# Flamingo block on one core: half of the probabilities of tiles 6 to 30 transposed by DMA

## The reference

```python
def xattn(x, context):                       # x: (2, 2048, 512), context: (2, 77, 384)
    q = (layernorm(x) @ Wq), k = context @ Wk, v = context @ Wv      # 16 heads of 32
    scores = einsum('bhid,bhjd->bhij', q, k) * 32 ** -0.5            # masked by context_mask
    return (softmax(scores) @ v).reshape(B, N, 512) @ Wo
def ffn(x):
    xq = fake_quant(layernorm(x))            # int8 steps, one scale from max |x| of the tensor
    h = fake_quant(silu(xq @ wq(w_gate).T) * (xq @ wq(w_up).T))      # wq: int8 per row
    return h @ wq(w_down).T
x = x + tanh(g_xattn) * xattn(x, ctx)
x = x + tanh(g_ffn) * ffn(x)
```

## Time and profile before

| | |
|---|---|
| median of 3 runs | 635.77 us |
| profiled execution / its span | 635.47 / 633.7 us |
| TensorE, VectorE, ScalarE, GpSimd busy | 612.7, 509.5, 352.0, 193.2 us |
| stretch 190 to 240 us: TensorE, VectorE, ScalarE, GpSimd busy | 50.00, 43.91, 31.83, 17.80 of 50 us |
| granted clock of TensorE, 35 to 375 us | 1.00 |
| TensorE idle from the end of attention to its next weight load at 390.53 us | 4.25 us |

### The profile page before, as it was taken

How to read it: one execution, slowest core, us unless ns; L and a number is a source line. 1 busy time by engine, 2 the same in 40 slices (tenths; PEclk the granted TensorE clock), 3 DMA queues, 4 the chain that set the end, 5 groups by cost and what they waited for, 6 DMA issues and landing times. The chain is left out here.

```text
span 633.7 us, 12623 instructions
## 1 busy us (share of the span) xinstructions
PE 612.7 (97%) x3862; PEld 460.0 (73%) x3862; DVE 509.5 (80%) x954; ACT 352.0 (56%) x512; POOL 193.2 (30%) x416
## 2 busy tenths in 40 slices
PE   8899999999999999999999976999999999899997
PEld 6689999999999999999999864444444444444544
DVE  6588788888988888899888658788888888866764
ACT  5264566667566666756664343555555554365553
POOL 7121233333323333323321202111111110057775
PEclk9999999999999999999999998999999999999999
DMA  8839433222222223222411000276446110099623
GB/s 312 201 94 260 134 59 68 54 62 50 58 67 58 66 58 65 75 43 78 97 49 44 25 0 1 50 242 223 132 136 207 28 29 11 0 345 416 267 110 122
DMA packets 85206, 69.61 MB, mean 110 GB/s; under 512 B 64915, under 2 KB 67373, under 8 KB 85165
## 3 DMA queue, kind: packets, MB, share of 16 engines
q1 hardware_dynamic: 79377, 52.13, 29.8%
q10 hardware_dynamic: 5788, 16.98, 7.6%
HBM read 32.48 MB, written 21.36 MB: 85 GB/s over the span
## 5 line engine op out<-in xcount | busy, mean ns | idle before, releaser
L1342 ACT ACTIVATE sb_silu<-ps_g,sb_sgu 128x512 f32<-128x512 f32 x88 | 60.5, 687 | 72.1 <-PE ps_g L1429 42.7
L1429 PE MATMUL ps_g<-sb_xqT,sb_wgu 128*128 128x512 bf16 x352 | 90.3, 379 | 0.6 <-DVE sb_xqT L1385 0.6
L1429 PE MATMUL ps_u<-sb_xqT,sb_wgu 128*128 128x512 bf16 x352 | 90.3, 379 | 0.0
L1400 DVE SCALAR_TENSOR_TENSOR sb_h<-ps_u,sb_sgu,sb_silu 128x512 f32<-128x512 f32 (+1 forms) x88 | 66.0, 751 | 19.8 <-PE ps_u L1429 19.3
L1053 PE MATMUL ps_o<-sb_vblk,sb_pT 128*128 (+4 forms) x640 | 78.8, 270 | 2.4 <-ACT sb_pT L603 1.6
L1053 PEld LDWEIGHTS ps_o<-sb_vblk,sb_pT 128*128 128x128 f32 (+1 forms) x640 | 76.9, 191 | 3.3 <-ACT sb_pT L603 2.0
L986 PE MATMUL ps_q<-sb_xT_hi,sb_wq_hi 128*128 128x256 f32 x256 | 75.5, 295 | 0.0
L988 PE MATMUL ps_q<-sb_xT_hi,sb_wq_lo 128*128 128x256 f32 x256 | 72.3, 282 | 0.0
L987 PE MATMUL ps_q<-sb_xT_lo,sb_wq_hi 128*128 128x256 f32 x256 | 72.2, 282 | 0.0
L1635 PE MATMUL ps_z<-sb_wdT,sb_hq 128*128 128x512 bf16 x330 | 71.6, 379 | 0.0
L716 DVE TENSOR_REDUCE sb_smax<-ps_s 128x8 f32<-128x616 f32 x64 | 51.1, 798 | 23.6 <-PE ps_s L1031 21.4
(11 more groups left out here) (227 smaller groups left out, 1325.7 us busy)
## 6 DMA issues: line engine op xcount, KB each, us to landing
h_spill<-sb_h SPq DMA_DIRECT2D x4, 2816.0 KB, 8.8
sb_h<-h_spill ACTq DMA_DIRECT2D x16, 704.0 KB, 7.1
out_dram<-sb_wgu SPq DMA_DIRECT2D x31, 256.0 KB, 2.0
sb_x<-in_x_dram ACTq DMA_DIRECT2D x1, 4096.0 KB, 19.4
sb_w_in<-in_L_ffn_w_gate_dram SPq DMA_DIRECT2D x11, 256.0 KB, 2.6
sb_w_in<-in_L_ffn_w_up_dram SPq DMA_DIRECT2D x11, 256.0 KB, 2.6
sb_x<-in_x_dram SPq DMA_DIRECT2D x2, 1024.0 KB, 14.7
sb_x<-in_x_dram SPq DMA_DIRECT2D x2, 512.0 KB, 4.9
```

What stands on the lines that cost most here:

```text
L1342: act.activation(silu[(j * KI + i) % 2][:, :, :].rearrange("p t n -> p (t n)"), p_g[(j * KI + i) % 2][:, :], ACT.Silu, scale=sgu[:, i:i + ...
L1400: dve.scalar_tensor_tensor(steps_h, p_u[(j * KI + i) % 2][:, :, :], sgu[:, KI + i:KI + i + 1], silu[(j * KI + i) % 2][:, :, :], ALU.mult, ...
L1429: last = pe.matmul(banks[(j * KI + i) % 2][:, :], wgu[:, what, k, i * P:(i + 1) * P], xqT[j][:, k, :], start=(k == 0), stop=(k == KD - 1))
```

## The change

For tiles 6 to 30 (`by_dma`) half 0 of the probabilities is not transposed by TensorE. GpSimd splits the 616 words into two planes of 16-bit halves, padded to 640 (`prob_split`, after a small product into `carry`), SyncE transposes the planes with a DMA of 128 x 1280 (`prob_transposed`), and ScalarE joins them into `sb_pT` (`prob_join`). Half 1 stays on TensorE, as do both halves of tiles 0 to 5 and 31, now in two pieces of five transposes instead of three of four, four and two. `sb_prob` has one buffer; the subtraction of half 0 waits for the split of the tile before it. The second half of the outputs goes to a second bank, which it shares with the fifth transpose. On TensorE both halves of the outputs follow both halves of the scores and queries. On VectorE the reduction for the second layer norm moves ahead of the maximum of half 1, and the division of the outputs' first half moves behind the queries' low part. The hardware loop covers slots 8 to 19.

```diff
-CHUNKS = [(0, 4), (4, 8), (8, 2 * KB)]
+PROB0, PROB1 = 6, NT - 1
+PW = KB * P
...
-prob = [sb(f"prob{i}", [P, 2, HW]) for i in range(2)]
-pT = sb("pT", [P, 2 * KB, P])
+prob = sb("prob", [P, 2, HW])
+pT_u = sb("pT", [P, 2 * KB * P * 2], U16)
+pT = pT_u[:, :].bitcast(F32).rearrange("p (k n) -> p k n", n=P)
+ppl_u = sb("ppl", [P, 2, 2 * PW], U16)
...
-p_p = [pb(f"p{i}", [P, 4, P]) for i in range(2)]
+p_pp = pb("p", [P, 8, P])
+p_p = [p_pp[:, 0:4, :], p_pp[:, 4:8, :]]
 p_ob = pb("o", [P, 512])
-p_o = p_ob[:, 0:HH * VW].rearrange("p (h d) -> p h d", h=HH)
+p_o = [a[:, 0:HH * VW].rearrange("p (h d) -> p h d", h=HH)
+       for a in (p_ob, p_pp[:, KB:8, :].rearrange("p k n -> p (k n)"))]
...
+def by_dma(n):
+    return not isinstance(n, int) or PROB0 <= n < PROB1
+def turned(n, half):
+    if by_dma(n):
+        return PROB0 + n + 1
+    return 2 * n + half + 1 - (PROB1 - PROB0 if n >= PROB1 else 0)
...
-        slot(n, n)
-    with eng.Fori(1, 5) as i:
+    for n in range(8):
+        slot(n, n % 4)
+    with eng.Fori(2, 5) as i:
...
+    def prob_transposed(n):
+        if n == PROB0:
+            sp.wait_ge(g_zero, 9)
+        sp.wait_ge(g_ppl, n - PROB0 + 1)
+        sp.wait_ge(a_p, 2 * n)
+        sp.dma_start_transpose(ppl_u[:, 1, :].rearrange("p (c n) -> p c n", n=P),
+                               ppl_u[:, 0, :]).then_inc(d_pT, 16)
...
+    def prob_split(n):
+        wait(pool, a_exp, 2 * n + 1)
+        wait(pool, d_pT, 16 * (n - PROB0))
+        pool.tensor_tensor(carry[:, :], eps[:, :], minus[:, :], ALU.mult)
+        pool.tensor_copy(ppl_planes[:, :, 0:HW], prob_pairs).then_inc(g_ppl, 1)
...
+            pool.wait_ge(t_v, B)
+            pool.memset(ppl_pads, 0.0).then_inc(g_zero, 1)
+        if runs(n, NT) and by_dma(n):
+            prob_split(n)
...
+    def exponential(n, half):
+        wait(act, v_sub, 2 * n + half + 1)
+        act.activation(prob[:, half, :], prob[:, half, :], ACT.Exp, scale=SCALE).then_inc(a_exp, 1)
+    def prob_copy(m, half):
+        wait(act, t_p, turned(m, half))
+        wait(act, t_o, 2 * m - 1 + half)
+        act.copy(pT[:, half * KB:(half + 1) * KB, :], p_pp[:, 0:KB, :]).then_inc(a_p, 1)
+    def prob_join(m):
+        wait(act, d_pT, 16 * (m - PROB0) + 16)
+        wait(act, t_o, 2 * m - 1)
+        act.copy(pT_pairs, ppl_T).then_inc(a_p, 1)
...
-        for c, (k0, k1) in enumerate(CHUNKS):
-            if c == 2 and runs(n - 4, NT - 1):
-                wait(act, g_nb2, n - 3)
-                wait(act, v_xmax, n - 3)
-                if isinstance(n, int) and n >= PLANES_FREE:
-                    act.wait_ge(v_xlo, NT)
-                else:
-                    wait(act, v_x1, n - 2)
-                act.activation(xabs(n - 4), row(n - 4), ACT.Abs, bias=nb2[:, span(n - 4)],
-                               scale=rs2[:, span(n - 4)]).then_inc(a_abs, 1)
-            if runs(n - 1, NT):
-                wait(act, t_p, 3 * (n - 1) + c + 1)
-                wait(act, t_o, 2 * (n - 1) - (c == 0))
-                act.copy(pT[:, k0:k1, :], p_p[c % 2][:, 0:k1 - k0, :]).then_inc(a_p, 1)
-        for half in range(2):
-            if runs(n, NT):
-                wait(act, v_sub, 2 * n + half + 1)
-                act.activation(prob[t % 2][:, half, :], prob[t % 2][:, half, :], ACT.Exp,
-                               scale=SCALE).then_inc(a_exp, 1)
-            if half == 0 and runs(n + 2, NT):
-                q_part(n + 2, (t + 2) % 4)
+        if runs(n - 1, NT):
+            if not by_dma(n - 1):
+                prob_copy(n - 1, 0)
+            prob_copy(n - 1, 1)
+        if runs(n - 4, NT - 1):
+            wait(act, g_nb2, n - 3)
+            wait(act, v_xmax, n - 3)
+            if isinstance(n, int) and n >= PLANES_FREE:
+                act.wait_ge(v_xlo, NT)
+            else:
+                wait(act, v_x1, n - 2)
+            act.activation(xabs(n - 4), row(n - 4), ACT.Abs, bias=nb2[:, span(n - 4)],
+                           scale=rs2[:, span(n - 4)]).then_inc(a_abs, 1)
+        if runs(n, NT):
+            exponential(n, 0)
+        if runs(n - 1, NT) and by_dma(n - 1):
+            prob_join(n - 1)
+        if runs(n + 2, NT):
+            q_part(n + 2, (t + 2) % 4)
+        if runs(n, NT):
+            exponential(n, 1)
...
-        wait(dve, t_p, 3 * (n - 1))
+        if isinstance(n, int) and n == 0:
+            dve.wait_ge(t_ck, 1)
+        elif half == 0 and by_dma(n - 1):
+            wait(dve, g_ppl, n - PROB0)
+        else:
+            wait(dve, t_p, turned(n - 1, half))
         dve.tensor_tensor(
-            prob[t % 2][:, half, :].rearrange("p (g h m) -> p g h m", g=2, h=HG), half_scores(),
+            prob[:, half, :].rearrange("p (g h m) -> p g h m", g=2, h=HG), half_scores(),
...
+        dve.reciprocal(rden[:, half, :], p_o[half][:, :, HD]).then_inc(v_rec, 1)
...
         dve.tensor_tensor(o_sb[:, half * HH * HD:(half + 1) * HH * HD]
-                          .rearrange("p (h d) -> p h d", h=HH), p_o[:, :, 0:HD],
+                          .rearrange("p (h d) -> p h d", h=HH), p_o[half][:, :, 0:HD],
...
             dve.bn_aggr(mvt[:, :], bn2[:, 0, :]).then_inc(v_st2, 1)
-        if runs(n - 1, NT):
-            outputs_rec(n - 1, 0)
+        if runs(n - 4, NT):
+            wait(dve, a_abs, n - 3)
+            dve.tensor_reduce(xmax[:, span(n - 4)], xabs(n - 4), X, ALU.max).then_inc(v_xmax, 1)
+        if runs(n, NT):
+            scores_max(n, 1)
         if runs(n, NW):
...
             dve.reciprocal(w_inv[:, :], w_am[:, :]).then_inc(v_winv, 1)
-        if runs(n - 1, NT):
-            outputs_norm(n - 1, 0)
         if runs(n, NT):
-            scores_max(n, 1)
+            scores_sub(n, t, 1)
         if runs(n, NW):
...
         down_part(n, 1)
-        if runs(n - 4, NT):
-            wait(dve, a_abs, n - 3)
-            dve.tensor_reduce(xmax[:, span(n - 4)], xabs(n - 4), X, ALU.max).then_inc(v_xmax, 1)
-        if runs(n, NT):
-            scores_sub(n, t, 1)
         if isinstance(n, int) and n == 0:
...
             dve.wait_ge(v_v, 2 * B)
-            dve.memset(p_p[1][:, 0, :], 0.0).then_inc(v_zero, 1)
+            dve.memset(p_pp[:, KB - 1, :], 0.0).then_inc(v_zero, 1)
...
         if runs(n - 1, NT):
+            outputs_rec(n - 1, 0)
+            outputs_norm(n - 1, 0)
...
-        wait(pe, a_exp, 2 * n + (1 if c == 0 else 2))
-        wait(pe, a_p, 3 * n + (0, -1, 1)[c])
+    def prob_transpose(n, half):
+        wait(pe, a_exp, 2 * n + half + 1)
+        wait(pe, a_p, 2 * n + (half and not by_dma(n)))
+        wait(pe, v_o, 2 * n)
         if isinstance(n, int) and n == 0:
             pe.wait_ge(v_zero, 1)
-        k0, k1 = CHUNKS[c]
-        for k in range(k0, k1):
-            half, j = divmod(k, KB)
-            last = pe.transpose(p_p[c % 2][0:ROWS[j], k - k0, :],
-                                prob[t % 2][:, half, P * j:P * j + ROWS[j]], identf[:, :])
+        for j in range(KB):
+            last = pe.transpose(p_pp[0:ROWS[j], j, :], prob[:, half, P * j:P * j + ROWS[j]],
+                                identf[:, :])
         last.then_inc(t_p, 1)
...
     def outputs(n, half):
-        wait(pe, a_p, 3 * n + 2 + half)
-        wait(pe, v_o, 2 * n + half)
+        wait(pe, a_p, 2 * n + (2 if by_dma(n) else 1 + half))
+        wait(pe, v_o, 2 * n - 1 + half)
         b = n // (S // P)
...
             last = pe.matmul(
-                p_o[:, first:end + 1, :].rearrange("p h d -> p (h d)"),
+                p_o[half][:, first:end + 1, :].rearrange("p h d -> p (h d)"),
...
-        prob_transpose(n - 1, (t - 1) % 4, 0)
-        prob_transpose(n - 1, (t - 1) % 4, 1)
+        prob_transpose(n - 1, 0)
         out_transpose(n - 2)
         project(n - 3, [0])
-        prob_transpose(n - 1, (t - 1) % 4, 2)
+        prob_transpose(n - 1, 1)
...
         if runs(n - 1, NT):
-            prob_transpose(n - 1, (t - 1) % 4, 0)
-            prob_transpose(n - 1, (t - 1) % 4, 1)
+            prob_transpose(n - 1, 1 if by_dma(n - 1) else 0)
         if runs(n + 2, NT):
             queries(n + 2, (t + 2) % 4, 0)
-        if runs(n - 1, NT):
-            outputs(n - 1, 0)
-            prob_transpose(n - 1, (t - 1) % 4, 2)
-        if runs(n, NT):
+        if runs(n - 1, NT) and not by_dma(n - 1):
+            prob_transpose(n - 1, 1)
+        early = isinstance(n, int) and n < 2
+        if early:
             scores(n, t, 1)
...
             queries(n + 2, (t + 2) % 4, 1)
+        if runs(n, NT) and not early:
+            scores(n, t, 1)
         if runs(n - 1, NT):
+            outputs(n - 1, 0)
```

More of the change, by code:

```diff
@@ L93, in flamingo_block @@
         sb, _, sem = tensors(top)
+        t_warm = sem("t_warm")
         x1 = sb("x1", [P, NT, D])
@@ L185, in flamingo_block @@
                 xpl_T = xpl[:, :].rearrange("p (k n) -> p k n", k=KD)
+                prob_pairs = prob[:, 0, :].bitcast(U16).rearrange("p (n two) -> p two n", two=2)
+                ppl_planes = ppl_u[:, 0, :].rearrange("p (two n) -> p two n", two=2)
```

(26 more changed lines are left out.)

14 lines of the change are left out of this document (6 added, 8 removed).

## The result

The changed kernel takes 642.45 us (median of 4 runs, 640.87 to 646.1), the kernel before, run beside it, 635.9 (635.01 to 636.42). The ratio is 1.0104 with an interval of 1.0072 to 1.0135: slower by 1.0%. Its profiled execution took 640.87 us, with a span of 639.1 and a mean granted clock of 0.984. Those of before were 635.47, 633.7 and 0.997. Three executions in the experiments were slower than the rest of their kernel (experiment 1 at 641.84, experiment 7 at 756.84, the kernel before at 897.26): they stand in the medians and ranges, but not in the ratios.

A forecast was written before the change was run, and what follows sets the result against it. The prediction took TensorE, full in the attention slots, as the bound; gains of 5.5 us less costs of 0.5, 1.0 and 1.5, and -0.2 at the end, gave -2.7 us, so 632.9 us, range 629.3 to 636.3.

The forecast's parts named there:

- The chain in the slot: Attention slots: outputs wait for subtraction, exponential and join, 0.35 us in the loop, 0.25 outside; gain 5.5 us, not 12.5.
- The start: Slots 0 to 6: same work on TensorE, so 0 us (-0.5 to +0.5).
- The loads of w_down: Slots 24 and 26: GpSimd's later cast delays the loads and VectorE waits for them; cost 1.0 us (0 to 3).
- VectorE's own lack of slack: Slots 22 and 24: VectorE has nothing left, so slots 23 and 25 start their chain 0.26 late; costs 0.5 us.
- The shared port: Rival, slots 23 and 25: GpSimd's split holds VectorE's quantisation up by 1.1 us each; 634.6 us, no chance of its own.
- The end: Slots 30 and 31 have no queries, so the join's wait shows: slot 30 +1.5 us, slot 31 on -0.2 us.
- rival D: Waits in slots 30 and 31 make TensorE's clock fall: +5 to +10 us, so 640; chance 0.07.
- these waits are each well under 4 us, with matmuls between: Slots 30 and 31: argument that waits of 1.7, 1.3 and 0.9 us would not make the clock fall.
- the term of 0 for the clock: End of attention: the forecast's sum held no time for a fall of TensorE's clock.
- The sum: Whole kernel: -5.5 + 0.5 + 1.0 + 1.5 - 0.2 = -2.7 us, forecast at 632.9.

The follow-up runs named there:

- experiment 1: The changed kernel with ScalarE's join of the last tile's planes ahead of the exponential of half 0: 634.06 us, ratio 0.9961.
- experiment 7: The kernel before, with ScalarE repeating its first copy of transposed probabilities in slots 30 and 31 so the outputs wait longer: 642.93 us, ratio 1.0098.
- experiment 4: The changed kernel without the DMA path: TensorE makes all ten transposes, all engines in the new order: 640.79 us, ratio 1.008.
- experiment 8: Experiment 4 with TensorE's outputs of half 0 and scores of half 1 back in the old order, other engines in the new: 643.34 us, ratio 1.0108.
- Experiment 3: The changed kernel with dummy matmuls filling TensorE's waits in slots 30, 31 and 32: 637.52 us, ratio 1.0022.
- experiment 2: The changed kernel with tiles 29 and 30 also transposed by TensorE, not by DMA: 635.96 us, ratio 1.0009.
- experiment 6: Experiment 5 with tiles 29 and 30 transposed by TensorE: 629.04 us, ratio 0.9885.
- experiment 5: Experiment 1 with the three loads of the next w_down block behind the block's first store in SyncE's queue: 627.8 us, ratio 0.9889.

## Why the prediction was wrong

The forecast was 632.9 us with a range to 636.3. Its steps, in turn:

**The chain in the slot: right, and too short by a fifth of a microsecond.** The subtraction ends 3.60 after the slot's start (3.61 forecast), the join takes 1.65 as forecast, its planes have long landed (the transposing DMAs land in 3.3 us, against 3.1 in the earlier trace rows). But the exponential starts at 3.73 (3.64 forecast), where the Abs ahead of it on ScalarE ends, and the join's end reaches TensorE 0.12 later and not 0.05. In the loop the outputs load at 6.10, not 5.97. Everything behind takes 4.91, not 4.87, 0.03 of it in outputs half 0 (1.11 in place of 1.08). So the wait is 0.39 against 0.35, and the period 11.01 to 11.06, not 10.85: slots 8 to 19 win 0.0 us where 2.3 stood. Outside the loop the period is 10.79 to 10.81 against 10.75.

**The start: right in its number by luck, wrong in its reason.** Giving slots 0 to 6 "the same work on TensorE: 0" left out that the order changes for every slot. Slots 3 to 6 lost 0.07 or 0.08 each, and experiments 4 and 8 put most of that down to the seams of TensorE's order. Slot 1 lost 0.78 (9.14 against 8.36), with a wait ahead of the scores of half 1 that the kernel before has not:

```profile
37.56 0.19 PEld L1096 LDWEIGHTS ps_s<-sb_k_hi,sb_q_hi 128*128 128x128 f32 x1 [0.81 <-issue]
```

Slot 0, on the other side, began 1.09 earlier in this profile (25.12 against 26.21), at the end of a wait for a DMA, and that start lies anywhere from 25.12 to 27.10 in the ten profiles. The two cancel: slot 7 starts at 99.95 in both kernels.

**The loads of w_down: wrong in this kernel.** They were given 1.0 us and cost nothing. The cast did start later in its slot, as forecast, and the last load of the block with it. But the forecast took the 5 us of the earlier trace rows for the landing. In the changed kernel VectorE began on the three loads 3.5 us after the last was issued and waited for none, so all had landed:

```profile
309.36 0.43 SPq L479 DMA_DIRECT2D sb_w_in<-in_L_ffn_w_down_dram  x1
```

```profile
312.85 0.67 DVE L821 TENSOR_REDUCE sb_wd_am<-sb_w_in 128x1 f32<-128x512 f32 x1
```

The mechanism came with experiment 1, where the split comes behind the join as well, at 2.85, 2.84 and 1.01 us of wait. Why the loads of the earlier trace rows took 5.3 us from the last issue is open. VectorE's own lack of slack was given 0.5 us; 0.2 came, for the reason that follows.

**The shared port: the hold came, the price was small.** In slot 25 of the changed kernel GpSimd's split and VectorE's first quantisation of w_down overlap:

```profile
301.90 1.21 POOL L537 COPY sb_ppl<-sb_prob 128x1232 uint16<-128x1232 uint16 x1
```

```profile
302.06 1.34 DVE L829 TENSOR_SCALAR sb_w_i<-sb_w_in,sb_wd_inv 128x512 int8<-128x512 f32 x1
```

Where the split came later, in experiment 1, the same instruction took its 0.48:

```profile
298.82 0.48 DVE L829 TENSOR_SCALAR sb_w_i<-sb_w_in,sb_wd_inv 128x512 int8<-128x512 f32 x1
```

It was held for 0.86 us, and ended 0.29 after the split. The Trainium skill (SBUF — State Buffer, Who interferes with whom) has it that a two-port VectorE operation and GpSimd block each other for the whole instruction: for this pair the trace agrees. The prediction argued from the earlier trace rows that no such thing happens, with a cast as the other party. Those rows can't tell: cast and quantisation overlap there by 0.17 us only, and the quantisation ended 0.30 after the cast, as the held one ended 0.29 after the split. VectorE's slack took most of it: slots 23 and 25 have 10.89 and 10.90 instead of 10.80.

**The end: the waits right, the clock wrong.** At full clock slot 30 was forecast at 10.74 and slot 31 to the last out transpose at 17.3. Experiment 3 has 10.76, and 27.13 from slot 31 to the feed-forward stage, against 27.14 before. In the changed kernel slot 30 took 12.31 and the last out transpose came 21.17 us after slot 31 began. That is rival D, which had a chance of 0.07 and the price of 5 to 10 us. The step that failed is "these waits are each well under 4 us, with matmuls between", and with it the term of 0 for the clock: it compared each wait with the one idle stretch of 4.25 us ahead of the earlier trace rows. In the changed kernel slot 30 had two waits, 1.66 and 1.35, and the clock fell behind the second. Experiments 2, 3 and 7 show it from three sides: without these waits no fall in the two slots, with the waits filled no fall, and with a wait of 2.87 and no change a fall. What length of wait it takes isn't shown; experiments 2, 4 and 6 have the same one in slot 32 with and without a fall.

**The sum.** -4.0 was forecast for the slots up to 30, -2.7 came. The waits of the end were forecast at +1.3, and 37.89 - 36.40 = +1.5 came. The clock, forecast at 0, was +5.2, and the rest of the kernel, forecast at 0, +1.4. No run shows that this last part is the change's. 0.3 of it lies in the gate and up products, at whose start the clock is half for 6.8 us and not 3.4; 0.6 lies from there to the last weight load and 0.5 behind it. A stretch of 3.4 us at half clock stands at the start of the down stage in seven of the ten profiles, in that of experiment 7 too, but in neither of the two that are compared, so it isn't in the 1.4. Why it comes and goes is open. So is how much of the spread between runs is clock: the changed kernel's own runs go with it, 641.08 at 0.985, 640.87 at 0.984, 643.82 at 0.981, 646.1 at 0.978.

## What to carry to other kernels

Work taken off a full engine pays only as far as the next chain allows: write down when each operand of the consumer is ready, and put the producer that hangs on nothing of this round ahead of the one that does. Here two lines on ScalarE and three loads in SyncE's queue turned a ratio of 1.010 into 0.989. And look at the rounds that have less cover than the others, the last ones above all: a wait that is hidden in the steady state is bare there, and here TensorE paid for it twice, 1.5 us as idle time and 5.2 us in clock.

## What had not been expected of the hardware

- The clock of TensorE fell under back-to-back matmuls, up to 2.3 us after the last wait had ended. Two idle pieces of 1.66 and 1.35 us in one slot, 0.9 us apart, or one of 2.87, brought a stretch at 1.2 GHz. Single ones of 1.02 to 1.05 in the same slots brought none, nor did 1.65 and 0.76 in experiment 5. One of 2.17 or 2.18 in slot 32 was followed by a stretch in experiments 4 and 6 and by none in experiment 2. The stretches in slots 30 to 32 lasted 3.4 us, or 10.2.
- A GpSimd copy of 16-bit planes (1.21 us) held an f32 to int8 TENSOR_SCALAR on VectorE for 0.86 us. A TENSOR_REDUCE beside the same copy (start 203.79, 0.68 us long) wasn't held.
- A ScalarE copy of 1280 16-bit columns takes 1.655 us and one of 1024 takes 1.344 (means of 25 and 24): 1.2 ns for each column more, against the 0.87 worked out from the f32 forms of the earlier trace rows.
